# Second edge stage of a graph network: gathered rows added by an identity product in PSUM instead of by a vector add

## The reference

```python
ms = src_s[edge_src] + dst_s[edge_dst]
mv = src_v[edge_src] + dst_v[edge_dst]
w = h @ rw3 + roff
w1, w2, w3, w4, w5 = jnp.split(w, [C0, 2 * C0, 2 * C0 + C1, 2 * C0 + 2 * C1], axis=1)
o0a = w1 * ms
o0b = w4 * (jnp.einsum('eud,ed->eu', mv, Y1) / SQ3)
o1a = (w2 * ms)[:, :, None] * Y1[:, None, :]
o1b = w3[:, :, None] * mv
o1c = w5[:, :, None] * (jnp.cross(mv, Y1[:, None, :]) / SQ2)
ls, lv = _eq_lin(ds, dv, lin_ws, lin_bs, lin_wv)
```

## Time and profile before

| | |
|---|---|
| device time, median of 3 runs | 10617.58 us (10607.35 to 10631.53) |
| span of the profiled execution | 10684.3 us |
| busy in it: PE, DVE, POOL, ACT | 84%, 75%, 63%, 45% |
| the second edge stage in it | from about 5650 to about 9940 us |
| PE and DVE busy in 5700 to 6700 us | 860.12 us, 847.58 us |
| PE's granted clock there | 0.97 |

### The profile page before, as it was taken

The page is one execution under the profiler, slowest core; times in us unless marked ns, Lnnn a source line. Parts: engine busy times, 40 slices in busy tenths (PEclk is TensorE's granted clock), DMA queues, the critical chain, the costliest instruction groups (busy, mean ns, idle before and its releaser), DMA issues. The chain is left out here.

```text
span 10684.3 us, 192482 instructions
## 1 busy us (share of the span) xinstructions
PE 8950.9 (84%) x34728; PEld 5257.6 (49%) x34728; DVE 8008.3 (75%) x15400; ACT 4828.6 (45%) x9073; POOL 6686.3 (63%) x4771
## 2 busy tenths in 40 slices
PE   0888888888888799999986888888888888888588
PEld 0444444444444222223225666666666666666233
DVE  3277777777777688888877888888888888888455
ACT  0276666666666211111113444444444444444255
POOL 4488888888888788888873444444444444444231
PEclk5599999999999899999988999999999999999699
DMA  5588888888888999999973444444444444444222
GB/s 202 172 168 171 168 163 169 165 166 169 167 163 162 208 228 224 223 233 230 227 165 105 121 121 121 120 124 124 121 121 122 121 126 121 120 121 123 56 68 52
DMA packets 1081323, 1616.13 MB, mean 151 GB/s; under 512 B 218498, under 2 KB 831885, under 8 KB 1025357
## 3 DMA queue, kind: packets, MB, share of 16 engines
q1 hardware_dynamic: 755862, 1273.87, 43.7%
q0 software_dynamic: 325056, 338.58, 20.2%
HBM read 1533.80 MB, written 444.07 MB: 185 GB/s over the span
## 5 line engine op out<-in xcount | busy, mean ns | idle before, releaser
L442 POOL DMA_INDIRECT sums<-e_total,e_place x1568 | 2493.7, 1590 | 584.8 <-DMA sums<-e_total,e_place 313.9
L1933 POOL DMA_INDIRECT e_rows<-TS,e_at x1568 | 1542.7, 984 | 1738.0 <-DVE e_m L1961 1174.4
L579 PE MATMUL ps<-e_win,e_pick 128*128 128x448 f32 x3136 | 1341.6, 573 | 159.6 <-DVE e_u L476 105.9
L579 PEld LDWEIGHTS ps<-e_win,e_pick 128*128 128x128 f32 x3136 | 620.4, 203 | 917.7 <-issue 832.9
L2261 ACT ACTIVATE e_dT<-ps 128x512 f32<-128x512 f32 x1176 | 671.1, 597 | 841.2 <-PE ps L2135 353.3
L2135 PE MATMUL ps<-ident,e_d 128*128 128x128 f32 x4704 | 663.1, 278 | 300.6 <-ACT e_dT L2261 289.6
L1917 POOL TENSOR_TENSOR e_val<-e_val 128x640 f32<-128x640 f32 x392 | 511.5, 1306 | 523.7 <-ACT e_val L2238 518.0
L1094 POOL TENSOR_TENSOR n_zv<-n_zv,n_ast 128x1536 f32<-128x1536 f32 x200 | 762.9, 3814 | 120.0 <-DMA n_zv<-in_x_groups 107.7
L1299 PE MATMUL ps<-n_z,w_uss 128*64 128x512 f32 x1600 | 748.6, 612 | 20.8 <-DVE n_z L1142 20.1
L2261 ACT ACTIVATE e_oT<-ps 128x512 f32<-128x512 f32 x784 | 469.1, 598 | 627.1 <-PE ps L2163 454.9
L2149 PE MATMUL ps<-e_val,e_q 128*128 128x168 f32 x3136 | 630.7, 327 | 127.6 <-ACT e_tot L2272 108.0
(11 more groups left out here) (438 smaller groups left out, 19874.2 us busy)
## 6 DMA issues: line engine op xcount, KB each, us to landing
e_win<-T SPq DMA_DIRECT2D x1568, 168.0 KB
n_z<-in_x_groups SPq DMA_DIRECT2D x400, 512.0 KB
n_zv<-in_x_groups SPq DMA_DIRECT2D x800, 192.0 KB
TOT<-e_tot SPq DMA_DIRECT2D x392, 352.0 KB
e_row<-in_src_rows SPq DMA_DIRECT2D x98, 1024.0 KB
e_local<-LR SPq DMA_DIRECT2D x196, 512.0 KB
e_row<-in_dst_rows SPq DMA_DIRECT2D x98, 1024.0 KB
e_win<-TD SPq DMA_DIRECT2D x1568, 60.0 KB
```

What stands on the lines that cost most here:

```text
L442: pool.indirect_dma_start(sums[c], bass.IndirectOffsetOnAxis(ap=place[:, r % 4, c:c + 1], axis=0), total[:, r % 4, c, 0:MSG0], None, compu ...
L579: pe.matmul(g[:, c, :], pick[:, p, R * c:R * c + R], win[:, s, c, :], start=True, stop=True).then_inc(spread, 1)
L1933: pool.indirect_dma_start(rows[:, p, 0, c, :], None, TS, bass.IndirectOffsetOnAxis(ap=at[:, gp, col:col + 1], axis=0)).then_inc(rows_here[ ...
```

## The change

The add moves from DVE to PE. The spread of each tile no longer ends its PSUM group: a second product, of the gathered rows with the identity matrix, is accumulated on top. PE therefore waits for the gathered rows ahead of the spread, and DVE no longer does. ACT's copy out of PSUM is now already the sum; it goes straight into `m_`, which is longer by two vector components: behind x, y, z a second copy writes x, y once more. So the rotated operands of the cross product are plain slices, and `cA` and `cB` take one instruction each. The semaphore `added` is gone. POOL (the gathers of step r) and SP (the index load) now wait for `spread`, of the same step as before; ACT's copy of step r waits for `d_ready` of step r-2, since `m_` of that step must have been read. PE computes the spread of step r in body r-2; DVE added step r in its body r-1.

```diff
--- before.py
+++ after.py
@@ -1750,8 +1750,8 @@
         row = sb("e1_row", [R, 2, 16 * R], I32)
         dh = sb("e1_dh", [128, 2, R], I32)
         hh = sb("e1_h", [128, 2, GT * R])
-        rows = sb("e1_rows", [R, 2, 2, GT, X])
-        m_ = sb("e1_m", [R, 2, GT, X])
+        rows = sb("e1_rows", [R, 2, GT, X])
+        m_ = sb("e1_m", [R, 2, GT, X + 2 * V])
         prod, cA, cB, cr = (sb("e1_" + n, [R, GT, 3, V]) for n in ("prod", "cA", "cB", "cr"))
         dot = sb("e1_dot", [R, GT, V])
         d = sb("e1_d", [R, 2, GT, 3, 128])
@@ -1771,8 +1771,8 @@
         asked = sem("e1_asked")
         blank, picked, spread, far_kept, q_ready = (sem("e1_" + n) for n in ("blank", "picked", "spread", "far_kept", "q_ready"))
         stored = [sem(f"e1_stored{s}") for s in range(STEPS)]
-        ones_set, added, crossed, mixed, w_ready, d_ready, turned, kept, mapped, outs, by_y, freed = (sem("e1_" + n) for n in (
-            "ones_set", "added", "crossed", "mixed", "w_ready", "d_ready", "turned", "kept", "mapped", "outs", "by_y", "freed"))
+        ones_set, crossed, mixed, w_ready, d_ready, turned, kept, mapped, outs, by_y, freed = (sem("e1_" + n) for n in (
+            "ones_set", "crossed", "mixed", "w_ready", "d_ready", "turned", "kept", "mapped", "outs", "by_y", "freed"))
         silued, logit, xT, apart, masked, forward, scanned, mT, shifted = (sem("e1_" + n) for n in (
             "silued", "logit", "xT", "apart", "masked", "forward", "scanned", "mT", "shifted"))
         exped, mkept, u_ready, summed, totkept = (sem("e1_" + n) for n in (
@@ -1874,7 +1874,7 @@
                             load_h(r % 2, t * 4 + (r // 2 + 1))
                         if r % 4 == 3 and not final:
                             gate(sp, k)
-                            sp.wait_ge(added, i.n(1, 1))
+                            sp.wait_ge(spread, i.n(2, 2))
                             load_at(r // 4, t + 1)
                         if r % 4 == 2 and not i.before(4) and not (final and r == 6):
                             gate(sp, k)
@@ -1925,12 +1925,12 @@
                             pool.wait_ge(at_here[gp], i.uses(16, 16))
                         if not i.before(2):
                             gate(pool, k)
-                            pool.wait_ge(added, i.n(1, 1, 2))
+                            pool.wait_ge(spread, i.n(2, 2, 2))
                         pool.sem_inc(begun, 1)
                         gate(pool, k)
                         for c in range(GT):
                             col = 4 * (r % 4) + c
-                            pool.indirect_dma_start(rows[:, p, 0, c, :], None, TS, bass.IndirectOffsetOnAxis(
+                            pool.indirect_dma_start(rows[:, p, c, :], None, TS, bass.IndirectOffsetOnAxis(
                                 ap=at[:, gp, col:col + 1], axis=0)).then_inc(rows_here[p], 16)
                         if not i.before(8):
                             weighted(i, 8)
@@ -1955,19 +1955,12 @@
 
                     p = i.r % 2
                     gate(dve, k)
-                    dve.wait_ge(rows_here[p], i.uses(256, 64 * (i.r // 2) + 64))
-                    gate(dve, k)
                     dve.wait_ge(far_kept, i.n(2, 2))
-                    dve.tensor_tensor(m_[:, p], rows[:, p, 0], rows[:, p, 1], ALU.add).then_inc(added, 1)
-                    gate(dve, k)
-                    dve.wait_ge(added, i.n(1, 1))
-                    vec = m_[:, p, :, S:X].rearrange("n c (i u) -> n c i u", i=3)
+                    vec = [m_[:, p, :, S + V * j:S + V * j + V3].rearrange("n c (i u) -> n c i u", i=3) for j in range(3)]
                     y = [bc(yx[:, j:j + 3, bass.ds(i.n(4), GT)].rearrange("n i c -> n c i"), V, 3) for j in range(3)]
-                    dve.tensor_tensor(prod[:], vec, y[0], ALU.mult)
-                    dve.tensor_tensor(cA[:, :, 0:2], vec[:, :, 1:3], y[2][:, :, 0:2], ALU.mult)
-                    dve.tensor_tensor(cA[:, :, 2], vec[:, :, 0], y[2][:, :, 2], ALU.mult)
-                    dve.tensor_tensor(cB[:, :, 0], vec[:, :, 2], y[1][:, :, 0], ALU.mult)
-                    dve.tensor_tensor(cB[:, :, 1:3], vec[:, :, 0:2], y[1][:, :, 1:3], ALU.mult).then_inc(crossed, 1)
+                    dve.tensor_tensor(prod[:], vec[0], y[0], ALU.mult)
+                    dve.tensor_tensor(cA[:], vec[1], y[2], ALU.mult)
+                    dve.tensor_tensor(cB[:], vec[2], y[1], ALU.mult).then_inc(crossed, 1)
                     gate(dve, k)
                     dve.wait_ge(crossed, i.n(1, 1))
                     dve.tensor_reduce(dot[:], prod[:].rearrange("n c i u -> n c u i"), AX.X, ALU.add)
@@ -2117,11 +2110,14 @@
                         pe.wait_ge(picked, i.n(1, 1))
                         gate(pe, k)
                         pe.wait_ge(win_here[s], i.uses(256, 128 * (i.r // 4) + 128))
+                        gate(pe, k)
+                        pe.wait_ge(rows_here[p], i.uses(256, 64 * (i.r // 2) + 64))
                     if after is not None:
                         gate(pe, k)
                         pe.wait_ge(*after)
                     for c in (2 * half, 2 * half + 1):
-                        last = pe.matmul(to[:, c % 2], pick[:, p, R * c:R * c + R], win[:, s, c, :], start=True, stop=True)
+                        pe.matmul(to[:, c % 2], pick[:, p, R * c:R * c + R], win[:, s, c, :], start=True, stop=False)
+                        last = pe.matmul(to[:, c % 2], I[:], rows[:, p, c, :], start=False, stop=True)
                     last.then_inc(spread, 1)
 
                 def turn(i, j):
@@ -2248,8 +2244,10 @@
                     act.wait_ge(spread, i.n(2, half + 1))
                     if half == 0 and not i.before(2):
                         gate(act, k)
-                        act.wait_ge(added, i.n(1, 1, 2))
-                    act.activation(rows[:, i.r % 2, 1, 2 * half:2 * half + 2, :], of, ACT.Copy).then_inc(far_kept, 1)
+                        act.wait_ge(d_ready, i.n(1, 1, 2))
+                    to = m_[:, i.r % 2, 2 * half:2 * half + 2]
+                    act.activation(to[:, :, 0:X], of, ACT.Copy)
+                    act.activation(to[:, :, X:X + 2 * V], of[:, :, S:S + 2 * V], ACT.Copy).then_inc(far_kept, 1)
 
                 def keep(i, j):
                     gate(act, k)
```

## The result

The changed kernel takes **10999.53 us** (median of four, 10994.4 to 11013.4) against 10616.4 us of the kernel before on the same chip (10607.35 to 10631.53): a ratio of **1.0361, 95% interval 1.0347 to 1.0376**, so 3.6% slower. The forecast was 11200 us in 10700 to 11420: right in sign, some 200 us too high.

The account below looks back on a forecast made before the run. Bound: PE completions held by POOL's gather bursts, in one step PE's floor. Four steps go from 43.2 to 47.5-50.9 us, by 98 +420 to +755 on 10617.6: middle 11200 us, own forecast 10950-11420, stated range 10700-11420.

Parts of the forecast that it names:

- A completion that falls late in a burst is held to about 5.9 us after its first gather: PE completions late in POOL's four gathers reach ACT only about 5.9 us after the first gather; early ones do not wait.
- the prediction's own sign of being wrong: Forecast wrong if completions 2.4 to 5.7 us into a burst reach ACT at once, or POOL starts elsewhere.
- Rival 3: Half a hold: held completions can come out between gathers, about 1 us late; 44.5 us for four steps, 10745 us; chance 0.12.
- The trigger moves the burst to T + 3.6: POOL's first gather comes 3.6 us after T, the start of PE's spread, releasing held completions at T + 9.5.
- The four kinds of step: Steps r = 4, 5, 6, 7 (and 0 to 3) forecast at 12.4, 10.1, 11.7, 13.3 us, 47.5 for four against 43.2.
- The delayed bursts: In r = 6 and 2, POOL runs late: one burst near T + 1, the next at once near T + 7.4.
- PE's +1.09 us a step, 427 in all: PE's eight added passes at 0.137 us lengthen PE's floor by 1.09 us a step, 427 us over 392 steps.
- DVE's saving worth 0: DVE sheds about 1.1 us a step, worth 0 on the step, since DVE's mean is 2.2 us below the period.
- The clock falls in two steps, 2 x 1.7: If PE's granted clock falls in two of four steps through standing idle, 2 x 1.7 us more, 50.9 for four.
- r = 7: Step r = 7 and 3: the last mapping's completion is held, the spread's second half 0.7 to 1.2 late; 13.3 us.
- Rival 2: PE alone: holds stay as they were and each step grows by PE's 1.09 us; 11045 us; chance 0.13.
- Rival 1: Faster: no completion that matters is held by bursts, PE's floor of 10.06 us a step decides; 10350 us; chance 0.13.

Follow-up runs that it names:

- e3: Kernel before, with only POOL's gathers also waiting for the spread of the step before (late trigger): 11107.9 us, ratio 1.0408.
- e5: e2 with POOL's multiply of each group's first step put behind the next step's gathers: 10334.4 us, ratio 0.9686 to the kernel before.
- e7: Changed kernel with POOL's gathers left out and the rows constant: 10211.2 us, ratio 0.9576 to the kernel before.
- e6: Kernel before with POOL's gathers left out and the rows constant: 10300.6 us, ratio 0.966.
- e2: Changed kernel with POOL's gathers also waiting for ACT's copy of turn 2 of step r-4 (earlier burst): 10421.0 us, ratio 0.9771 to the kernel before.
- e12: Changed kernel with one gather a step in place of four, the other rows constant, trigger kept: 10223.5 us, ratio 0.9576 to the kernel before.
- e4: Kernel before with every product of PE's spread issued twice: 10960.2 us, ratio 1.0267.
- e8: Kernel before with four gather buffers instead of two, e2's trigger and e5's placing of the multiply: 10539.2 us, ratio 0.9872.

## Why the prediction was right, and where it was off

*A completion that falls late in a burst is held to about 5.9 us after its first gather*: holds for most, at 5.79 and 5.86 in the changed kernel, 5.76 in e3, 5.89 in e5. It is causal: without gathers, with SP's loads or with one gather, the holds are gone and with them all or most of the time. As a rule without exception it is too strong, though, at both ends. The totals at 8009.55 came out 4.37 after the first gather. Turn 1 of the last step (the second four of the eight transposes at 8040.98) was done at 8042.02, only 2.01 into the burst, and was copied 1.62 late, at 8043.64. And by the prediction's own sign of being wrong, a completion between 2.4 and 5.7 us that reaches ACT at once, it has a counterexample: the first half of the spread in e5, on time at 2.87. What decides between these, no run shows. Rival 3's half hold exists; it didn't decide, since a second completion of the same step was held to the end.

*The trigger moves the burst to T + 3.6*: measured 3.59. The four kinds of step, forecast 12.4, 10.1, 11.7 and 13.3, were 13.62, 9.74, 11.47 and 13.83 in the four shown, 48.7, where the mean over the stage is 46.9; over 95 such fours of the trace the four kinds are 12.75, 9.73, 11.38 and 13.18 in the mean. The forecast's sum was 47.5, without any loss to the clock. The delayed bursts were where they were put, near T + 1 and T + 7.4 of r = 6 (T = 8024.95; these two are the first gathers of two bursts), and r = 5 has none:

```profile
8026.09 1.13 POOL L1933 DMA_INDIRECT e_rows<-TS,e_at  x1 [0.15 <-issue]
...
8032.42 0.99 POOL L1933 DMA_INDIRECT e_rows<-TS,e_at  x1 [0.16 <-issue]
```

*PE's +1.09 us a step, 427 in all*: the passes follow each other at the pitch that was said (products of two passes begin 0.27 apart, at 8001.59, 8001.86 and 8002.13). But their sum with the floor, 10.06, was too high: the step without a gather takes 9.74, and e7, where PE is busy throughout, 9.63. And "on PE's floor" with PE's floor as the floor of the kernel before was wrong. I took 8.97, the shortest of four steps, for what binds when nothing is held. e6 has 9.85 a step, and DVE busy 96% of it. The short step was short because DVE had only 4.85 us of work in it and 12.42 in the one ahead: a floor can't be read from one step of a ring in which an engine's work spills into the next.

*DVE's saving worth 0*: it was worth more than that in floor, and less in size than the -1.1 I gave. Without gathers the changed kernel's floor is 9.63 against 9.85, so the change pays 0.86 us in four steps where I had it cost 4.4. As to size, the prediction took 8.55 us of DVE work a step from four steps, where 847.58 of 1000 us over steps of 10.80 are 9.15; the changed kernel has 8.86 (2266.54 of 3000 over 11.73), not "near 7.4". The mean durations of what the change touched on DVE, before and after: the add 952 ns, the five products and the combination 2522, together 3474; now 811 + 552 + 560 + 876 = 2799. So 0.68 less, as the sum was built on medians; and of that the selection of the members, which the change didn't touch, takes 0.27 back (738 to 1012). POOL's multiply used to fall mostly beside the add; now it falls beside the first product (552 median, 1620 longest), the combination, whose mean went from 548 to 876, or that selection. Groups by line of before and then of after, and one such pair in the timeline of after:

```profile
L1961 DVE TENSOR_TENSOR e_m<-e_rows 128x640 f32<-128x640 f32 x392 | 373.3, 952 | 0.0
L2004 DVE TENSOR_TENSOR e_q<-e_row,dstI 128x512 f32<-128x512 int32 x392 | 289.3, 738 | 13.3 <-PE ps L2149 13.3
...
L1974 DVE TENSOR_TENSOR e_cr<-e_cA,e_cB 128x384 f32<-128x384 f32 x392 | 214.8, 548 | 0.0
```

```profile
L1997 DVE TENSOR_TENSOR e_q<-e_row,dstI 128x512 f32<-128x512 int32 x392 | 396.5, 1012 | 13.3 <-PE ps L2145 13.3
L1967 DVE TENSOR_TENSOR e_cr<-e_cA,e_cB 128x384 f32<-128x384 f32 x392 | 343.5, 876 | 0.0
L1961 DVE TENSOR_TENSOR e_prod<-e_m,yx 128x384 f32<-128x384 f32 x392 | 317.9, 811 | 17.0 <-issue 16.0 <-ACT e_m L2250 0.2
```

```profile
8037.35 1.99 DVE L1967 TENSOR_TENSOR e_cr<-e_cA,e_cB 128x384 f32<-128x384 f32 x1
...
8037.64 1.27 POOL L1917 TENSOR_TENSOR e_val<-e_val 128x640 f32<-128x640 f32 x1
```

The combination has two SBUF inputs as the add had. The Trainium skill's "SBUF — State Buffer", section "SBUF: two separate sides", says that whichever of such a pair starts first shuts the other out for its whole length. The trace agrees that the two shut each other out (1.99 against 0.55). It doesn't show the order: by these records DVE began 0.29 us ahead of POOL and was still the one that took long, and POOL's times are rough. The groups above show that taking away one VectorE operation didn't take away the wait, it handed it to its neighbours. The prediction read that page for the add alone.

*The clock falls in two steps, 2 x 1.7*: it does fall in two (0.88 in both), so this term was about right for the four shown: an estimate from the granted clock is (1 - 0.88) x (13.62 + 13.83) = 3.3 us. Over 6000 to 9000 us the clock is 0.96, by the same reckoning 1.9 us lost in four steps, where the kernel before with 0.97 loses 1.3. What was too long is the steps themselves. Without that loss the stage's four steps are 46.9 - 1.9 = 45.0 us, where the sum had 47.5. So the lower end of the forecast, +4.3 x 98 = 421 and 11040, lies near the measured +3.7 x 98 = 363 in the stage partly by luck: its steps are 2.5 us too long, and it leaves out a loss of 1.9. The largest part is r = 7, 13.3 where the step shown has 13.83 x 0.88 = 12.2 at full clock; a part in all four may be PE's floor, 10.06 in place of 9.63.

The balance in one line, for four steps: the kernel before takes 39.4 without gathers and 3.8 more with them, the changed kernel 38.5 and 8.4. The holds are the main part of the 3.8 and 8.4, but e5, with holds that cost little, is still 1.3 over e7, so not all of it need be holds. Rival 2, PE alone at 11045, lies nearer to the measured time than my middle, and the time alone couldn't have told them apart; e2, e5 and e12 do: with the same PE work the changed kernel beats the kernel before, once the burst lies elsewhere or is one gather. Rival 1's world is e5: no completion that matters falls into a burst, and the changed kernel is then faster than the kernel before by 3.1%, where 10350 against 10618 is 2.5%. The nearness is in part luck, since its floor was 10.06 a step and e5's steps take 9.96.

What stays open: e5 is 123 us over e7, with PE busy 2953 of 3000 us; no run says where these go. And e4's size: how much of its +296 is passes and how much moved bursts wasn't separated with the gathers in.

## What to carry to other kernels

When an edit changes what triggers a row of indirect DMAs on GpSimd, work out where in the consumer's step that row will lie before counting the instructions saved: here one wait was worth 443 us, and the compute edit about 89 the other way. Let such a row begin so that what completes from about 2 to 5.8 us after its start is something nobody waits for, or keep rows short (one gather held nothing here; two and three weren't run). When an operation of DVE is removed or a burst moved, look also at what POOL's multiply will then fall beside: in e8 that goes with most of the time over e6. Take an engine's floor from its busy time over hundreds of steps, or from a run with the suspect left out, not from the shortest step in sight.

## What the runs showed of the hardware

Many completions of PE that fall 2 to 5.8 us into a row of four indirect DMAs issued back to back by POOL (each 0.94 to 1.3 us, 0.3 apart) reach ACT late, by up to 3.3 us (done at 8042.59, copied at 8045.87), most of them 5.8 to 6.0 us after the first gather began (0.4 us after the last one ended in the step of e5, where two gathers were longer, 1.0 to 1.1 in the others shown), some earlier (3.63 and 4.37 us), and one kind, 2.87 us into the row in e5, on time. Fetching a tenth of the bytes leaves this as it is (11031 against 11000), one gather in place of four ends it (10223 against 10211 without any, equal ratios), and so do plain loads of the same size from SP (10394, no such wait left). The profile doesn't name it: it shows as a wait for "remote", or for a DMA of an earlier stage that used the same semaphore. Through what the completions are delayed, no run shows.

VectorE operations with two SBUF inputs take longer while POOL's multiply runs: 1.99 us in place of 0.55 for the combination in the changed kernel, and a mean of 1.61 in place of 0.71 for the selection of the members in e8 against e6.
